# A fused attention and feed-forward kernel: weight rounding, small steps and feed-forward order rearranged

## The chip, the cores and the metric

The kernel runs on one core of one Trainium2 chip. The metric is the device time of one execution in microseconds (us). The core has TensorE (PE, with PEld for its weight loads), VectorE (DVE), ScalarE (ACT), GpSimd (POOL) and SyncE (SP, which issues most DMAs). Every engine works through its own instructions in order; semaphores join them.

## The reference, cut to what matters

`x` and `ctx` are 64 batches of 128 rows by 256 columns. Four residual layers follow each other:

```
x = x + mlstm(layernorm(x), ctx, ctx, gates, out_w)        # 4 heads of 64, log-sigmoid forget gates, head norm
x = x + layernorm(x) @ (ternary(W0) * mean|W0|).T
x = x + softmax((layernorm(x) @ Wq) @ (ctx @ Wk).T / 16) @ (ctx @ Wv)
x = x + bitlinear(silu(bitlinear(h, Wg)) * bitlinear(h, Wu), Wd),  h = layernorm(x)

ternary(w)      = clip(round(w / mean|w|), -1, 1)
bitlinear(x, w) = act_quant(x) @ (ternary(w) * mean|w|).T
act_quant(x)    = round(x * 127 / max|x|) * max|x| / 127   # max over each row
```

Wg and Wu are 1024 x 256, Wd is 256 x 1024. So three large weights are rounded and clipped to -1, 0, 1 once, and in the last layer the rows are rounded twice: before gate and up (256 columns) and after the product (1024 columns).

## The kernel before, in words

The 64 batches are 16 groups of four. `schedule` writes out two opening turns and then 14 turns z = 0 to 13; turn z works on three groups at once: projections and gates of group z+2, decay, scores and heads of group z+1 (m), the two middle layers of group z. It also prepares the quantized rows of group z-1 (y) and stores those of z-2 (w) to a DRAM scratch, `rows_q`. Each engine has the stages of a turn in a fixed written order, and the eight PSUM banks go round in the order of `STAGES`. After turn 13 the last groups are drained, and then 64 feed-forward iterations i run, one per batch.

In a turn VectorE does: statistics of x (L1198), `cut_product`, statistics of group y, `x2_rows`, statistics, `head_sums` (L1321), `row_steps` for y (L1269: maximum, scale, inverse, factors for the way back), one pass of `ternary` (L1233), the gates (L1409 on: sum, negated, absolute value, copy, relu; then, after ScalarE's exp and log, `nlf`, L1421), `row_maxima`, `heads_out`, the running maximum and its splits, `x3_rows`, statistics. ScalarE does the gates' exp and log (L938, L940) behind its copies of stage T2 (L819), and the exponentials of the softmax (L852) behind those.

Weights: `ternary(n, step)` is three VectorE passes over 128 x 2048 floats for each of n = 1 (gate), 2 (up), 3 (down): scale and round, minimum, maximum into a 16-bit tile. Two passes stand in the second opening turn, one in each of turns 0 to 6 (`TERNARY_AT`). TensorE transposes the result in stages WG, WU, WD, at the end of turns 0, 3 and 6 (`WEIGHTS_AT`), and ScalarE copies it out.

Feed-forward iteration i: TensorE does gate and up (`gate_up`, L684 to L690), the transposes of product i-2 (`product_rows`, L699), down of i-3 (`down`, L707). ScalarE: silu (L989), copy of the transposed product i-2 (L993), scaled result of i-3 (L1000). VectorE: product of up and silu (L1513), its row maximum (L1516), step (L1523), its inverse `hscale` (L1526), then `last_rows(i)`, the remaining row work of groups 13 to 15. GpSimd: `hback` (L1145), rounding of the product (L1152), sum with x (L1160). SyncE issues the transposing reads of `rows_q` four iterations ahead and one store of 512 KB for each group, the last one after all four batches are done (L464). The product has two buffers (halves of C), the rounded one too.

## Time and profile before

| | us |
|---|---|
| three timed runs | 701.86, 703.54, 704.52 (median 703.54) |
| the profiled execution's own time | 703.04 |
| its span | 701.3 |
| opening turns, to the first x1 (0 to 47.03) | 47.03 |
| turns 0 to 13 (47.03 to 453.94) | 406.91 |
| draining of the last groups (453.94 to 491.29) | 37.35 |
| feed-forward, first to last product (491.29 to 689.34) | 198.05 |
| after the last product (689.34 to 701.3) | 11.96 |

The boundaries are starts of VectorE's instruction L1359 (x1 of a group; one per turn) and of L1513 (one per feed-forward iteration). 1.7 us of the execution's time lie outside the span.

### The profile page before, as it was taken

The numbers are of one execution on the slowest core, as the hardware profiler recorded it, in microseconds if no ns is written. First come the engines' busy times: TensorE is split into PE (matmuls) and PEld (weight loads), VectorE is DVE, ScalarE is ACT, GpSimd is POOL, SyncE is SP. The second block draws the span as 40 slices with busy tenths as digits, with TensorE's granted clock in tenths as the row PEclk, the third lists the DMA queues.
The fourth block names the chain that finished last, engine by engine and source line by source line (L and its number), as shares of the span: only waits on it lengthen the run. The fifth ranks groups of instructions, "written<-read, shape, count | busy, mean of one in ns | idle before, by whom it ended". The sixth has DMA issues, their size and how long they took to land.

```text
span 701.3 us, 15286 instructions
## 1 busy us (share of the span) xinstructions
PE 655.5 (93%) x4958; PEld 493.9 (70%) x4958; DVE 609.0 (87%) x1661; ACT 518.3 (74%) x1203; POOL 391.8 (56%) x556
## 2 busy tenths in 40 slices
PE   5889999999999999999999999998899999999996
PEld 4668778686867868788787787876465666666664
DVE  4787989888898887989889889897999999999994
ACT  4556677686767668787777787865588889888885
POOL 3366564362735445574574555652366667666665
PEclk9999999999999999999999999999999999999999
DMA  8310202122020312202212121014123424425221
GB/s 290 102 44 18 91 1 92 48 74 90 17 92 16 91 46 76 91 16 91 77 47 91 45 78 61 17 56 155 50 85 94 143 79 122 120 81 158 84 78 61
DMA packets 72659, 55.54 MB, mean 79 GB/s; under 512 B 20093, under 2 KB 72318, under 8 KB 72582
## 3 DMA queue, kind: packets, MB, share of 16 engines
q1 hardware_dynamic: 64134, 50.37, 23.7%
q10 hardware_dynamic: 8448, 4.20, 2.0%
q8 instruction: 42, 0.69, 0.4%
q14 instruction: 35, 0.29, 0.1%
HBM read 29.39 MB, written 20.97 MB: 72 GB/s over the span
## 4 chain that ended last, share of the span: by engine, by line
PE 53%; DVE 30%; ACT 10%; issue 4%; POOL 1%; DMA 1%; DVEq 0%; POOLq 0%; ACTq 0%
PE bank L690 10%; PE bank L637 8%; PE bank L658 8%; PE bank L607 5%; PE bank L707 5%; DVE C L1513 4%; DVE hmax L1516 4%; DVE st L1200 3%; PE bank L679 3%; PE bank L699 3%; PE bank L575 3%; ACT ew L852 2%; PE bank L566 2%; PE bank L512 2%; DVE x L1359 2%
## 5 line engine op out<-in xcount | busy, mean ns | idle before, releaser
L690 PE MATMUL bank<-WGU,fqT 128*128 128x512 bf16 x512 | 125.0, 382 | 4.0 <-DVE C L1513 3.4
L1074 POOL TENSOR_SCALAR_AFFINE_SELECT D<-D 128x512 f32<-128x512 f32 x64 | 38.4, 636 | 124.9 <-ACT D L843 124.9
L1059 POOL TENSOR_TENSOR rs<-ve,minus_half 128x4 f32<-128x4 f32 x64 | 65.3, 1026 | 47.5 <-DVE ve L1206 47.0
L1513 DVE SCALAR_TENSOR_TENSOR C<-bank,fback,D 128x1024 f32<-128x1024 f32 x64 | 81.9, 1280 | 7.4 <-ACT D L989 5.5
L690 PEld LDWEIGHTS bank<-WGU,fqT 128*128 128x128 bf16 x512 | 48.0, 98 | 57.0 <-DVE C L1513 17.3
L989 ACT ACTIVATE D<-bank,fback 128x1024 f32<-128x1024 f32 x64 | 71.1, 1111 | 15.6 <-PE bank L690 15.3
L1516 DVE TENSOR_REDUCE hmax<-C 128x1 f32<-128x1024 f32 x64 | 78.1, 1220 | 2.2
L993 ACT ACTIVATE fhT<-bank 128x1024 f16<-128x1024 f16 x64 | 65.5, 1023 | 19.5 <-PE bank L699 18.2
L1152 POOL TENSOR_SCALAR wtmp<-C,hscale 128x1024 f32<-128x1024 f32 x64 | 71.6, 1119 | 0.4 <-issue 0.4
L707 PE MATMUL bank<-WD,fhT 128*128 128x256 f16 x512 | 66.3, 273 | 0.3 <-ACT fhT L993 0.3
L1200 DVE BATCH_NORM_STATS2 st<-x 128x6 f32<-128x256 f32 x180 | 63.1, 413 | 2.6
L658 PE MATMUL bank<-W0T,x1T 128*128 128x256 f32 x256 | 59.3, 385 | 5.2 <-DVE C L1311 5.2
L637 PEld LDWEIGHTS bank<-vaug,C 128*128 128x128 f32 x512 | 61.6, 194 | 2.3 <-issue 1.6
L637 PE MATMUL bank<-vaug,C 128*128 128x65 f32 x512 | 61.6, 274 | 1.3 <-DVE C L1311 1.3
L607 PE MATMUL bank<-WX,qcT 128*128 128x268 f32 x256 | 62.0, 395 | 0.0
L575 PE MATMUL bank<-qcT,GT 128*128 128x512 f32 x128 | 60.6, 597 | 0.8 <-ACT GT L945 0.8
L1086 POOL TENSOR_TENSOR hr<-hv,minus_half 128x16 f32<-128x16 f32 x16 | 50.5, 3158 | 18.1 <-DVE hv L1340 18.1
L1145 POOL TENSOR_SCALAR hback<-hstep,mean_abs 128x1 f32<-128x1 f32 x64 | 17.2, 268 | 76.1 <-DVE hscale L1526 61.6
L658 PEld LDWEIGHTS bank<-W0T,x1T 128*128 128x128 f32 x256 | 47.3, 190 | 13.9 <-DVE C L1311 7.6
L1080 POOL TENSOR_TENSOR hh<-us,head_scale 128x256 f32<-128x256 f32 x64 | 43.4, 685 | 23.3 <-ACT usq L835 15.3
L1117 POOL TENSOR_TENSOR vaug<-cg,vg 128x256 f32<-128x256 f32 x64 | 50.7, 819 | 8.3 <-ACT vg L888 7.7
L607 PEld LDWEIGHTS bank<-WX,qcT 128*128 128x128 f32 x256 | 47.3, 190 | 11.0 <-issue 3.0
(198 smaller groups left out, 1514.2 us busy)
## 6 DMA issues: line engine op xcount, KB each, us to landing
out_dram<-x SPq DMA_DIRECT2D x31, 512.0 KB, 3.3
xg<-in_x_dram SPq DMA_DIRECT2D x16, 512.0 KB, 3.9
cg<-in_ctx_dram SPq DMA_DIRECT2D x16, 512.0 KB, 4.5
rows_q<-fq ACTq DMA_DIRECT2D x16, 256.0 KB, 2.2
xg<-out_dram SPq DMA_DIRECT2D x8, 512.0 KB, 5.1
cg<-out_dram SPq DMA_DIRECT2D x8, 512.0 KB, 5.0
raw<-in_L_ffn_w_gate_dram SPq DMA_DIRECT2D x1, 1024.0 KB, 7.9
nrm<-in_L_ffn_w_up_dram SPq DMA_DIRECT2D x1, 1024.0 KB, 10.3
```

What stands on the lines that cost most here:

```text
L575: mm = pe.matmul(o[:, :], GT[:, c, rows_at * P:(rows_at + 1) * P], turned[:, EC + c, :, :].rearrange("p b t -> p (b t)"), start=(c == 0), ...
L607: mm = pe.matmul(o[:, 0:VG], qcT[p][:, EC + c, b, :], WX[:, c, :], start=(c == 0), stop=(c == EC - 1))
L637: mm = pe.matmul(o[:, h * AUG:(h + 1) * AUG], C[:, b, h, :], vaug[q][:, b, h, :], start=True, stop=True)
L658: mm = pe.matmul(o[:, 0:E], x1T[:, b, c * P:(c + 1) * P], W0T[:, c, :], start=(c == 0), stop=(c == EC - 1))
L690: mm = pe.matmul(ps[k + half], fqT[:, s, c, :], WGU[:, c, which, half * 512:(half + 1) * 512], start=(c == 0), stop=(c == EC - 1))
L707: mm = pe.matmul(o[:, 0:E], fhT[:, s % 2, c * P:(c + 1) * P], WD[:, c, :], start=(c == 0), stop=(c == IC - 1))
L989: act.activation(fsil[:, s % 2, :], gate, ACT.Silu, scale=fback[:, p, s % FB, 0:1]).then_inc(g_clear, 1)
L993: act.activation(fhT[:, s % 2, :], bank_h[s % 2], ACT.Copy, bias=-OFFSET).then_inc(h_clear, 1)
L1152: pool.tensor_scalar(fhr[:, s % 2, :], fh[:, s % 2, :], hscale[:, s % FB:s % FB + 1], CODE, ALU.mult, ALU.add).then_inc(f_hr, 1)
L1200: dve.bn_stats(st[i][:, b, :], src[:, b, :]).then_inc(stats[i], 1)
L1513: dve.scalar_tensor_tensor(out=fh[:, s % 2, :], in0=up, scalar=fback[:, p, s % FB, 1:2], in1=fsil[:, s % 2, :], op0=ALU.mult, op1=ALU.mult ...
L1516: dve.tensor_reduce(hmax[:, s % FB:s % FB + 1], fh[:, s % 2, :], AX.X, ALU.max, apply_absolute_value=True).then_inc(f_hm, 1)
```

## The change: what it does

- Weights: ScalarE scales and rounds (`weight_rounded`, with the constant CODE so that the low 16 bits hold the value plus 1536); VectorE clips in one pass (`clip`); TensorE transposes the low halves; the copies out subtract 1536. Rounding of 1 and clip 1 stand in the second opening turn, 2 and 3 in turn 0; WG, WU, WD in turns 0, 1, 2.
- Gates: absolute value and relu move to ScalarE, ahead of exp and log.
- Smaller VectorE: one instruction fewer in `head_sums` (the factor 1/64 goes into `head_scale`), two fewer in `row_steps`; the `ve` of statistics 3 moves to GpSimd, ahead of its power.
- Feed-forward: TensorE's order is gate(i), transposes(i-2), up(i), down(i-3). VectorE keeps maximum and reciprocal (a guard column of 1e-5 stands in for the step's maximum); GpSimd multiplies by 127 and by mean/127. The product's buffers are tiles of `vg`.
- Last rows: spread over more iterations, statistics of group 14 before the feed-forward, x3 of group 15 two batches at a time; `rows_q` of groups 13 to 15 stored by SyncE. GpSimd scales two heads before `power(3)` in the draining. The last group is stored batch by batch.

```diff
-WEIGHTS_AT = {0: "WG", 3: "WU", 6: "WD"}
-TERNARY_AT = {0: (1, 2), 1: (2, 0), 2: (2, 1), 3: (2, 2), 4: (3, 0), 5: (3, 1), 6: (3, 2)}
+WEIGHTS_AT = {0: "WG", 1: "WU", 2: "WD"}
...
-        fh = flat(C).rearrange("p (i n) -> p i n", i=2)
+        fh = [flat(vg[k])[:, 0:INNER + 1] for k in (1, 2)]
... sync
+            for s in range(FB):
+                sp.wait_ge(f_done, B - FB + s + 1)
+                sp.dma_start(out[B - FB + s, :, :], fo[(NG - 1) % 2][:, s, :]).then_inc(f_last, 16)
... tensor
+            for i in range(B):
+                if i > 0:
+                    gate_rows_in(i)
+                if i in (2, 3):
+                    last_rows_out(i - 2)
+                if i > 1:
+                    product_rows(i - 2, i % 2)
+                if i > 0:
+                    up_rows_in(i)
+                if i in (3, 4):
+                    last_rows_out(i - 1)
+                if i > 2:
+                    down(i - 3)
... scalar
+                def weight_rounded(n):
+                    if n == 1:
+                        act.wait_ge(means_ready, 1)
+                    act.activation(w_raw[n], w_raw[n], ACT.Identity, scale=mean_inv[:, n:n + 1],
+                                   bias=magic[:, 0:1]).then_inc(w_round, 1)
...
                 if "W0" in bank.stages:
                     weight_copies("W0")
+                    weight_rounded(1)
+                if z == 0:
+                    weight_rounded(2)
                 if y is not None:
                     normalise_rows(y)
...
                 if n is not None:
-                    act.wait_ge(gstep, 4 * n + 3)
+                    act.wait_ge(gstep, n + 1)
+                    act.activation(gabs[:, :, :], gates[:, :, NH:], ACT.Abs).then_inc(g_exp, 1)
+                    act.activation(gneg[:, :, :], gates[:, :, NH:], ACT.Relu, scale=-1.0)
+                    act.wait_ge(g_exp, 2 * n + 1)
                     act.activation(gexp[:, :, :], gabs[:, :, :], ACT.Exp, scale=-1.0).then_inc(g_exp, 1)
...
+                if z == 0:
+                    weight_rounded(3)
                 if y is not None:
                     scale_rows(y, (0, 1))
... gpsimd
+                if i == 3:
+                    pool.wait_ge(aggr[3], GB * group + GB)
+                    pool.tensor_scalar(ve[3][:, :], mv[3][:, :, 1], LN_EPS, 1.0, ALU.add, ALU.mult).then_inc(veps[3], 1)
...
+            def product_scales(i):
+                s = i % FB
+                pool.wait_ge(f_hinv, i + 1)
+                pool.tensor_scalar(hscale[:, s:s + 1], hinv[:, s:s + 1], 127.0, None, ALU.mult).then_inc(f_hs, 1)
+                if i >= FB:
                     pool.wait_ge(o_clear, i - 1)
+                pool.tensor_scalar(hback[:, s:s + 1], hmax[:, s:s + 1], mean_abs[:, 3:4], 1.0 / 127.0,
                                    ALU.mult, ALU.mult).then_inc(f_hback, 1)
... vector
+            def clip(n):
+
+                dve.wait_ge(w_round, n)
+                dve.tensor_scalar(w_raw[n], w_raw[n], CODE + 1.0, CODE - 1.0, ALU.min, ALU.max).then_inc(tern, 1)
...
                 if "WS" in bank.stages:
-                    ternary(1, 0)
-                    ternary(1, 1)
+                    clip(1)
+                if z == 0:
+                    clip(2)
                 if y is not None:
                     row_steps(y)
-                if z in TERNARY_AT:
-                    ternary(*TERNARY_AT[z])
...
+                if z == 0:
+                    clip(3)
                 if z is not None:
                     inverse(bank, z)
                     x3_rows(bank, z, x2, x3)
...
-                for group, src, at in ((NG - 3, None, 1), (NG - 2, x3, 7), (NG - 1, x3_last, 24)):
+                for group, at in ((NG - 3, 2), (NG - 2, 20), (NG - 1, 38)):
+                    if i in range(at, at + 2 * GB, 2):
+                        row_max(group, ((i - at) // 2,))
```

## Rows read from the trace of the kernel before

**Rows 1.** Busy time by turn: stretch, length, then busy us (instructions) per engine, TensorE's granted clock.

```profile
47.03:453.94 406.91, 387.87 (x2958) 313.53 (x2957) 356.40 (x1163) 300.40 (x853) 223.70 (x294) 0.98 0.20 61
...
103.95:133.60 29.65, 27.78 (x210) 22.05 (x210) 26.56 (x85) 21.57 (x63) 15.27 (x21) 1.00 0.19 64
133.60:164.37 30.77, 29.29 (x210) 23.24 (x210) 26.98 (x86) 21.49 (x63) 15.38 (x21) 0.94 0.20 61
...
256.88:286.92 30.04, 29.35 (x221) 23.84 (x222) 24.69 (x84) 23.27 (x65) 15.64 (x21) 0.94 0.20 63
...
426.11:453.94 27.83, 26.97 (x211) 22.00 (x211) 24.61 (x84) 21.72 (x63) 16.14 (x22) 1.00 0.15 49
...
491.29:689.34 198.05, 194.07 (x1484) 122.81 (x1484) 187.46 (x317) 165.05 (x207) 127.71 (x190) 0.99 0.34 97
```

**Rows 2.** The chain of waits through a late turn, 334 to 364: start, us, what.

```profile
339.41 0.22 ACT gexp L938
...
339.65 0.23 ACT glog L940
...
339.97 0.40 DVE nlf L1421
...
340.89 0.28 DVE rawmax L1346
```

**Rows 3.** The chain of waits through turn 1, 74 to 106.

```profile
98.04 1.20 DVE nrm L1236
```

**Rows 4.** TensorE in order of time, end of turn 2.

```profile
133.15 1.62 PE L674 MATMUL bank<-ident,ew 128*128 128x128 f32 x4 [0.67 <-ACT ew L852]
```

**Rows 5.** ScalarE in order of time: the copies of stage WG.

```profile
77.46 1.94 ACT L884 ACTIVATE WGU<-bank 128x1024 bf16<-128x1024 f16 x2 [1.67 <-PE bank L535]
```

**Rows 6.** The draining, in order of time.

```profile
467.80 2.61 POOL L1080 TENSOR_TENSOR hh<-us,head_scale 128x256 f32<-128x256 f32 x4
...
467.93 0.60 DVE L1326 SCALAR_TENSOR_TENSOR hn<-us 128x16 f32<-128x16 f32 x1
```

**Rows 7.** Start of the feed-forward, in order of time.

```profile
491.29 1.28 DVE L1513 SCALAR_TENSOR_TENSOR C<-bank,fback,D 128x1024 f32<-128x1024 f32 x1 [3.56 <-ACT D L989]
...
494.32 1.66 DVE L1371 SCALAR_TENSOR_TENSOR qn<-bank,einv,hh 128x256 f32<-128x256 f32 x4
```

**Rows 8.** Last iterations of the feed-forward, all engines, in order of time.

```profile
686.17 0.26 POOL L1145 TENSOR_SCALAR hback<-hstep,mean_abs 128x1 f32<-128x1 f32 x1 [0.83 <-DVE hscale L1526]
...
686.30 1.28 DVE L1513 SCALAR_TENSOR_TENSOR C<-bank,fback,D 128x1024 f32<-128x1024 f32 x1
...
686.41 1.12 POOL L1152 TENSOR_SCALAR wtmp<-C,hscale 128x1024 f32<-128x1024 f32 x1
...
687.08 1.89 PE L690 MATMUL bank<-WGU,fqT 128*128 128x512 bf16 x8
...
688.14 1.11 ACT L989 ACTIVATE D<-bank,fback 128x1024 f32<-128x1024 f32 x1 [0.34 <-PE bank L690]
...
688.80 0.61 PE L699 MATMUL bank<-ident_h,wtmp 128*128 128x128 f16 x8
688.87 0.15 DVE L1523 TENSOR_SCALAR hstep<-hmax 128x1 f32<-128x1 f32 x1
689.06 0.16 DVE L1526 RECIPROCAL hscale<-hstep 128x1 f32<-128x1 f32 x1
...
689.25 1.04 PE L707 MATMUL bank<-WD,fhT 128*128 128x256 f16 x8
...
690.63 0.62 PE L699 MATMUL bank<-ident_h,wtmp 128*128 128x128 f16 x8 [0.34 <-POOL wtmp L1152]
...
697.92 0.37 SPq L464 DMA_DIRECT2D out_dram<-x  x1
```

**Rows 9.** DMA issues: what, count, KB each, median us to landing.

```profile
out_dram<-x SPq DMA_DIRECT2D x31, 512.0 KB, 3.3
...
rows_q<-fq ACTq DMA_DIRECT2D x16, 256.0 KB, 2.2
```

More of the change, by code:

```diff
@@ L15 @@
 IC = INNER // P
+HEAD_ROOT = 8.0
 AUG = DH + 1
@@ L369, in build @@
         fore, aft = last_places()
-        def feed_forward(eng, turn, behind={}):
-            for g in range(NG):
-                turn(g, g % 4, g == 0, g == NG - 1)
-                if g in behind:
-                    behind[g]()
         @block.sync
@@ L437, in _ @@
             sp.dma_start(grp(out, NG - 1), x3_last[:, :, :]).then_inc(x_out, 16)
-            def rows_written(g):
-                def wait():
-                    sp.wait_ge(q_out, 16 * (g + 1) + 16)
-                return wait
-            def written():
-                sp.wait_ge(x_out, 16 * NG)
-            def turn(g, p, first, last):
-                for s in range(FB):
-                    i = FB * g + s
-                    if not last:
-                        hold("sp", sp, u_full, i + 1)
-                        rows_turned(i + FB, s)
-                    if s == FB - 1 and not first:
-                        sp.wait_ge(f_done, FB * g)
-                        sp.dma_start(grp(out, g - 1), fo[(p + 1) % 2][:, :, :]).then_inc(f_out[(p + 1) % 2], 16)
-                        if g + 3 < NG:
-                            q = (p + 3) % 4
-                            sp.dma_start(fx[q], grp(out, g + 3)).then_inc(f_in[q], 16)
@@ new lines, in ffn_block @@
+            def ffn_block(i):
+                if i + FB < B:
+                    hold("sp", sp, u_full, i + 1)
+                    rows_turned(i + FB, i % FB)
+                if i % FB == FB - 1 and i >= FB:
+                    group_out(i // FB - 1)
+            for i in range(B):
+                for g, at in ((NG - 3, 18), (NG - 2, 36), (NG - 1, 54)):
+                    if i == at:
+                        sp.wait_ge(f_q, g + 1)
+                        sp.dma_start(grp(rows_q, g), fq[:, :, :]).then_inc(q_out, 16)
+                if i == FB * (NG - 6):
+                    sp.wait_ge(x_out, 16 * NG)
+                for g in range(NG - 3, NG):
+                    if i == FB * (g - 1):
+                        sp.wait_ge(q_out, 16 * (g + 1) + 16)
+                ffn_block(i)
@@ L1132, in _ @@
             power(2, NG - 1)
+            power(3, NG - 2)
+            shifts(3, NG - 2)
             def last_rows(i):
-                for group, at in ((NG - 2, 12), (NG - 1, 29)):
-                    if i == at:
-                        power(3, group)
-                        shifts(3, group)
-            def scale_back(i, s):
-                if not isinstance(i, int) or i > 3:
+                if i == 25:
+                    pool.wait_ge(f_n, GB * (NG - 1))
+                    power(3, NG - 1)
+                if i == 27:
+                    shifts(3, NG - 1)
@@ L1162, in ffn_turn @@
-            def ffn_turn(g, p, first, last):
-                for s in range(FB):
-                    i = FB * g + s
-                    scale_back(i, s)
-                    ffn_round(i, s)
-                    if s > 2:
-                        ffn_out(i - 3, s - 3, g, p)
-                    elif not first:
-                        ffn_out(i - 3, s + 1, g - 1, (p - 1) % 4)
-                    last_rows(i)
-            feed_forward(pool, ffn_turn)
-            for s in range(1, FB):
-                ffn_out(B - FB + s, s, NG - 1, 3)
+                pool.tensor_tensor(fo[g % 2][:, s, :], fy[:, i % 2, :], fx[g % 4][:, s, :], ALU.add).then_inc(f_done, 1)
@@ L1178, in _ @@
+            for i in range(B):
+                product_scales(i)
+                ffn_round(i)
+                if i > 2:
+                    ffn_out(i - 3)
+                last_rows(i)
+            for i in range(B - 3, B):
+                ffn_out(i)
         @block.vector
@@ L1390, in turn @@
                     means(bank)
-                    for step in range(3):
-                        ternary(0, step)
+                    ternary_w0()
                 if y is not None:
@@ L1528, in ffn_turn @@
-            def ffn_turn(g, p, first, last):
-                for s in range(FB):
-                    i = FB * g + s
-                    ffn_mul(i, s, g, p % 2)
-                    row_scale(i, s)
-                    if s == 1 and not last:
-                        scales(g + 1, 1 - p % 2)
-                    last_rows(i)
-            feed_forward(dve, ffn_turn)
+                dve.reciprocal(hinv[:, s:s + 1], hmax[:, s:s + 1]).then_inc(f_hinv, 1)
+            for k in range(2):
+                dve.memset(fh[k][:, INNER:INNER + 1], Q_EPS).then_inc(f_guard, 1)
@@ L1541 @@
+            for i in range(B):
+                ffn_mul(i)
+                if i % FB == 1 and i < B - FB:
+                    scales(i // FB + 1, (i // FB + 1) % 2)
+                last_rows(i)
 _INS = ['x', 'ctx_1024', 'L0_xattn_igate_w', 'L0_xattn_igate_b', 'L0_xattn_fgate_w', 'L0_xattn_fgate_b',
```

316 lines of the change are left out of this document (146 added, 170 removed).

## The prediction

> **What bounds the kernel now.** First the busy time by stretch. In the late turns TensorE is busy 26.97 of 27.83 us and VectorE 24.61; in turns with a pass of `ternary` the turn is longer (29.65), and where the clock column says 0.94 longer still (30.77) [rows 1]. So an early turn pays for more than the late one, and the late one is near TensorE's own limit. The feed-forward is 198.05 us for 63 iterations, 3.14 each, with both TensorE (194) and VectorE (187) nearly full [rows 1]. Then the chain of waits, to see which engine's work is really in the path. In a late turn it goes through ScalarE's exp and log to `nlf`, then through VectorE's `rawmax`, with one engine behind the other in every step [rows 2], and stays on VectorE through heads, splits, `x3_rows` and statistics until `cut_product` frees the banks of the next large product. The three or four small VectorE steps ahead of `nlf` are not in it: VectorE waits there for ScalarE. In turn 1 the pass of 1.20 us is in the chain [rows 3]. Last, the order of time in the feed-forward, to see who is late: TensorE starts gate at 687.08, the transposes at 688.80, down at 689.25 and has no gap; its own work takes 1.72 + 0.45 + 0.88 = 3.05 [rows 8]. VectorE's products start at 686.30 and, with the silu of 688.14 ending at 689.25, again near 689.34. VectorE itself could go round faster: the reciprocal starts 2.76 after the product (689.06 - 686.30), and the next product could follow about 0.11 later, 2.87. One row maximum of about 0.3 more makes 3.18, above TensorE's 3.05; that is where 3.14 comes from.
>
> **Opening turns.** `head_sums` loses a step of 0.2 in the chain; two passes become one, but the chain waits there for GpSimd's power. I take -0.4 (bounds -1.5 to +1).
>
> **Turns 0 to 13, weights.** These take 406.91 now [rows 1]. At the late pace of 27.83, thirteen intervals are 361.8, and the first, without a y group, is 26.85: 388.6. So 18.3 us is what weights cost today, for seven passes of about 1.2 (8.4), three transposing stages, and the low clock. After: clip 3 lies in the chain once (+1.2, [rows 3] for the length; it stands between the splits and `x3_rows`, which all lead to `cut_product`). Clip 2 stands where turn 0 waited for the projections: 0, as its cover is TensorE's projection; +1.2 if that cover is gone. WG, WU and WD add some 0.3 each while TensorE waits for VectorE anyway: +0.9 (bounds 0 and 2.2 each, the latter being 30.04 - 27.83 [rows 1], which also holds a low clock). ScalarE's three passes: the nearest row is 1.94 for 2 x 1024 elements [rows 5], so 1.94 each. Two stand in the slot that `normalise_rows` fills in later turns, and empty here, or beside queued copies; the third pushes the exponentials of turn 0 by 0.5, under VectorE's splits. I take +0.2 for all; bounds 0 and 5.8. The low clock: 30.77 - 29.65 = 1.1 a turn in four turns [rows 1], all with the wait of 0.67 ahead of the transposes of `ew` [rows 4]; I expect it gone. Sum of weights after: 1.2 + 0.9 + 0.2 = 2.3, so -16.0.
>
> A rule of the Trainium skill speaks against this part: "ScalarE: Activation LUTs", "Rules for kernel authors", puts relu, max, min, add and mul on VectorE rather than ScalarE. The rows agree on the length of one pass (1.94 against 1.20 [rows 3, 5]). They differ on what counts: ScalarE is busy 21.6 of 29.65, VectorE 26.6. By the rule the three passes would cost +5.8 and the time would be near 690; it is weighed as a rival below.
>
> **Gates.** Abs and relu on ScalarE stand behind the same copies and ahead of exp. Relu is pipelined; exp has to wait for abs, and one such dependent step is 339.65 - 339.41 = 0.24 [rows 2]. VectorE gives up three steps of 0.2, but it waited for the log anyway, so nothing comes back. `nlf` starts 0.25 late; of that the last `rawmax` had 0.07 of slack: it starts 0.18 late and everything behind it too. 13 turns x 0.18 = +2.3 (bounds -0.2 a turn, if the copies come earlier, and +0.3). The lighter `head_sums`, `row_steps` and `ve` save VectorE about 0.5 a turn, but lie ahead of the wait for the log: 0. The trace has no abs and no relu on ScalarE; the table sets are a risk (below). Turns together: -16.0 + 2.3 = -13.7.
>
> **Draining.** VectorE's four small steps of `head_sums` take 0.60 each beside GpSimd's 2.61 us of head scaling [rows 6], and 0.2 elsewhere. With two of the four scalings moved ahead of the power, about two of these steps fall back to 0.2, and one step goes: -1.0 (bounds -1.8 and 0). The statistics of group 14 (1.9 us) come in where VectorE waits 3.56 us for the first silu [rows 7]: 0, and +1.9 if that wait is gone.
>
> **Feed-forward.** Start: between product 0 and product 1 stand the four x3 rows, 494.32 to 495.98, so that the second comes 4.8 after the first (491.29) [rows 7]; two at a time makes 3.76 (2.68, 0.25 for the inverse, 0.83) and then 3.5. VectorE after: reciprocal at 2.57, next product at 2.68, with one row step 2.99, under 3.05. So its extras are free, and TensorE's 3.05 remains. But the new order makes a loop that had slack before: the transposes of product i now stand ahead of up(i+2). Its parts: up to product 1.06, as gate to silu (688.14 - 687.08); product to transposes 690.63 - 686.30 = 4.33 as a chain today; from this one VectorE step of 0.19 goes (689.06 - 688.87), and GpSimd's multiplication by 127 comes in with 0.24 (686.41 - 686.17, hback to rounding) plus the handoff, so +0.2, 4.53; transposes 0.45 (689.25 - 688.80). All [rows 8]. 1.06 + 4.53 + 0.45 = 6.04 in two iterations against TensorE's 6.10. It just fits, with nothing to spare. Before, the same transposes stood one up later and had 1.3 us. So now whatever delays one product or rounding is paid in full: three times ScalarE's conversion of a group's rows (1.05 us; silu 0.4 late), once GpSimd's power (1.0 us): I take 3 x 0.36 + 0.6 + 0.7 for small ones = 2.4. Product 0 to 63: 3.76 + 3.5 + 3.0 + 3.1 + 59 x 3.05 + 2.4 = 195.7, against 198.05: -2.4. Bounds: -5 (no delay paid) and, if the loop takes 6.3 rather than 6.04, +3.5.
>
> **End.** From the last product to its transposes +0.2. The last store starts at 697.92 and carries 512 KB; such stores land in 3.3 us, 256 KB of `rows_q` in 2.2 [rows 8, 9]. 1.1 less for half the size puts 128 KB near 1.7; the three before it are still on the queue, so I take -1.2 (bounds 0 and -1.7).
>
> **Sum.** -0.4 - 13.7 - 1.0 - 2.4 + 0.2 - 1.2 = -18.5 on the profiled execution's 703.04: 684.5. The median of the runs is 0.5 above that execution, so 685.0.
>
> **Rivals.** (a) The feed-forward loop is too long: the handoffs between three engines are worth 0.1 to 0.2 more per iteration than the rows of a relaxed loop say, and VectorE's row steps are then paid again. For it: 6.04 against 6.10. Against: every part is a row. 63 x 0.12 = +7.5, 692.5. (b) ScalarE's passes, clip 2 and the three transposing stages are in the path, as they are put close together: 5.8 + 1.2 + about 1 = +8, 693. For it: ScalarE's order is fixed and vg copies and exponentials stand behind each pass; against: its slots in turn 0 were partly empty. (c) The other side: a clock drop in every turn. Place: the transposes of `ew`. The longer gate chain delays the exponentials in all turns; TensorE waits, and a part of the turn then goes at the lower of its two levels, 1.2 instead of 2.4 GHz, as the clock column's 0.94 says of turns today [rows 1]. Price: 1.1 for the drop and about 0.6 for the wait in each of 14 turns, 23.8, 708.5. It decides when the wait reaches the 0.67 us of [rows 4]; the late turns, with 0.18 more, should stay under it. (d) The change does not do what it says: abs or relu needs another activation table: two loads a turn at 1.28 us, the length of the profile's two table loads, 14 x 2.56 = +36, 721. The same page of the Trainium skill ("Table sets: the hidden batching unit") says that cheap functions such as relu and abs are in every set, and prices a switch at about 2.7 us; no run here shows it. (e) Everything fits: extras in the feed-forward hidden, the gate chain's 0.18 absorbed, -5 more: 680.
>
> **How the numbers follow.** Forecast 0.58, (a) 0.14, (b) 0.12, (c) 0.05, (d) 0.02, (e) 0.09. The forecast's own range is 681 to 690. From 679 to 696, (e), (a) and (b) are in and about 0.15 is left out. A measurement of this kernel tells 0.5% (3.5 us) from no change: faster needs under 700.0. All but (c), (d) and mixtures of (a) and (b) with a partial (c) are faster: 0.92, same 0.03, slower 0.05.
>
> **What would show it.** Turns 3 to 13 at 28.0, clock 1.00; turn 1 near 29.4; `nlf` still waiting for the log, its wait longer; no table load in the turns; the feed-forward at 3.05 with jumps only at the three conversions and one power, GpSimd's rounding the last releaser of the transposes; the last store landing in about 2 us. Wrong if late turns fall below 27.8 (then VectorE's small steps were in the path), if turns stay at 29 or more, or if products stand 3.15 apart.

## The result

The changed kernel takes 684.0 us (median of 4 runs, 682.09 to 684.74) against 702.9 for the kernel before on the same chip: ratio 0.9725, 95% interval 0.9695 to 0.9755. Forecast were 685.0, range 679 to 696, faster. The profiled execution took 683.39, with a span of 681.4 (before 703.04 and 701.3).

| stretch | before | after | difference | forecast |
|---|---|---|---|---|
| opening, to the first x1 | 47.03 | 45.08 | -1.95 | -0.4 |
| turns 0 to 13 | 406.91 | 390.07 | -16.84 | -13.7 |
| draining, to the last x1 | 21.83 | 20.74 | -1.09 | -1.0 |
| last x1 to the first product | 15.52 | 17.06 | +1.54 | 0 |
| first to last product | 198.05 | 197.49 | -0.56 | -2.4 |
| after the last product | 11.96 | 10.96 | -1.0 | -1.0 |

(x1 and the product are the two instructions of VectorE whose starts mark the stretches; the last x1, that of group 15, begins at 475.77 in before: 453.94 to 475.77 and 475.77 to 491.29.)

Busy time by stretch in the kernel after, the same columns as [rows 1]: length, then busy us (instructions) of PE, PEld, DVE, ACT, POOL, granted clock, DMA share, GB/s. The rows are all turns, turn 1, turn 2, a late turn, and the feed-forward.

```profile
45.08:435.15 390.07, 379.83 (x2961) 309.03 (x2960) 330.49 (x1064) 304.85 (x883) 212.52 (x305) 1.00 0.20 63
71.39:100.59 29.20, 28.10 (x227) 22.88 (x226) 24.84 (x78) 22.04 (x64) 15.27 (x22) 1.00 0.17 56
100.59:129.45 28.86, 28.23 (x227) 23.04 (x226) 24.22 (x78) 23.46 (x67) 15.25 (x22) 1.00 0.20 65
213.54:241.17 27.63, 27.17 (x212) 22.04 (x211) 23.66 (x77) 21.64 (x65) 15.26 (x22) 1.00 0.23 67
472.95:670.44 197.49, 191.83 (x1485) 121.12 (x1484) 176.15 (x238) 164.76 (x208) 140.40 (x253) 1.00 0.34 97
```

Four readings. The clock is 1.00 in every turn, where four turns of before had 0.94 or 0.95. The turns reach the late pace (that of the turns in which no weight work is left) from turn 4 on, but for turn 8 with 28.21. That pace is 27.63, below the 27.84 of before, where the forecast had 28.0. In the feed-forward VectorE lost 11 us of work, TensorE 2, and the time barely moved.

### The profile page after: what moved, and what is told of

Read it like the earlier page. It is cut to its first block, busy times and chain, and to the rows that moved or that the text cites. A ratio compares the mean times of both kernels' runs of the same rounds, so it can differ in the third digit from the quotient of the medians.

```text
span 681.4 us, 15144 instructions
## 1 busy us (share of the span) xinstructions
PE 645.2 (95%) x4958; PEld 487.7 (72%) x4958; DVE 570.5 (84%) x1481; ACT 524.6 (77%) x1238; POOL 395.2 (58%) x636
## 4 chain that ended last, share of the span: by engine, by line
PE 68%; DVE 15%; ACT 10%; issue 3%; POOL 2%; DMA 1%; POOLq 0%; DVEq 0%; SPq 0%; ACTq 0%
PE bank L603 9%; PE bank L654 8%; PE bank L633 8%; PE bank L693 7%; PE bank L685 6%; PE bank L709 6%; PE bank L701 4%; PE bank L675 4%; ACT ew L853 4%; PE bank L508 3%; PE bank L571 3%; ACT x2T L820 2%; PE bank L562 2%; DVE st L1215 2%; PE bank L647 2%
## 5 line engine op out<-in xcount | busy, mean ns | idle before, releaser
L1520 DVE SCALAR_TENSOR_TENSOR vg<-bank,fback,D 128x1024 f32<-128x1024 f32 x64 | 82.1, 1283 | 18.2 <-PE bank L693 15.4
L1527 DVE TENSOR_REDUCE hmax<-vg 128x1 f32<-128x1025 f32 x64 | 78.1, 1221 | 2.2
L1172 POOL TENSOR_SCALAR wtmp<-vg,hscale 128x1024 f32<-128x1024 f32 x64 | 71.9, 1123 | 5.8
L685 PE MATMUL bank<-WGU,fqT 128*128 128x512 bf16 x256 | 65.7, 379 | 2.0 <-DMA fqT<-rows_q 1.6
L693 PE MATMUL bank<-WGU,fqT 128*128 128x512 bf16 x256 | 65.7, 379 | 0.0
L709 PEld LDWEIGHTS bank<-WD,fhT 128*128 128x128 f16 x512 | 49.9, 98 | 19.3 <-issue 0.6
L1099 POOL TENSOR_TENSOR hr<-hv,minus_half 128x16 f32<-128x16 f32 x16 | 46.5, 2905 | 14.8 <-DVE hv L1349 14.7
L867 ACT ACTIVATE qn<-xg,shift,rs 128x256 f32<-128x256 f32 x64 | 33.2, 593 | 26.9 <-POOL shift L1079 26.9
```

Of the source, the lines that this page charges most:

```text
L685: mm = pe.matmul(ps[bG + half], fqT[:, i % FB, c, :], WGU[:, c, 0, half * 512:(half + 1) * 512], start=(c == 0), stop=(c == EC - 1))
L693: mm = pe.matmul(ps[bU + half], fqT[:, i % FB, c, :], WGU[:, c, 1, half * 512:(half + 1) * 512], start=(c == 0), stop=(c == EC - 1))
L709: mm = pe.matmul(o[:, 0:E], fhT[:, i % 2, c * P:(c + 1) * P], WD[:, c, :], start=(c == 0), stop=(c == IC - 1))
L1172: pool.tensor_scalar(fhr[:, i % 2, :], fh[i % 2][:, 0:INNER], hscale[:, i % FB:i % FB + 1], CODE, ALU.mult, ALU.add).then_inc(f_hr, 1)
L1520: dve.scalar_tensor_tensor(out=fh[i % 2][:, 0:INNER], in0=up, scalar=fback[:, g % 2, s, 1:2], in1=fsil[:, i % 2, :], op0=ALU.mult, op1=ALU ...
L1527: dve.tensor_reduce(hmax[:, s:s + 1], fh[i % 2], AX.X, ALU.max, apply_absolute_value=True).then_inc(f_hm, 1)
```

## The experiments

Each was run four times, e1 to e4 on one chip and e5 to e12 on another, always beside the kernel before, whose median was 702.05, 702.22 and 702.80 in the three rounds. Kernels of different rounds are best compared by the ratio. The times of e2, e5, e6, e7 and e8 overlap the range of the kernel after; what these five show is read from the stretches of their profiled executions, one for each kernel. Boundaries are starts of the same instructions as above.

| kernel | us (range of 4) | ratio to before | opening | turns | to last x1 | to product 0 | products |
|---|---|---|---|---|---|---|---|
| before | | | 47.03 | 406.91 | 21.83 | 15.52 | 198.05 |
| after | 684.0 (682.1 to 684.7) | 0.9725 | 45.08 | 390.07 | 20.74 | 17.06 | 197.49 |
| e1 gates on ScalarE | 693.32 (692.5 to 694.0) | 0.9868 | 45.56 | 395.90 | 22.17 | 17.05 | 199.45 |
| e2 gates back on VectorE | 683.96 (683.7 to 685.1) | 0.9742 | 47.20 | 389.50 | 20.42 | 17.04 | 197.17 |
| e3 weights alone | 688.10 (687.6 to 688.7) | 0.9795 | 46.53 | 391.11 | 21.82 | 15.52 | 199.88 |
| e4 old order of TensorE | 680.84 (680.1 to 681.6) | 0.9697 | 45.34 | 389.96 | 20.74 | 17.05 | 194.24 |
| e5 early reads | 682.36 (681.8 to 684.5) | 0.9711 | 48.41 | 389.43 | 20.74 | 16.91 | 196.16 |
| e6 last group whole | 684.25 (683.9 to 685.3) | 0.9746 | 45.90 | 390.14 | 20.73 | 15.52 | 197.55 |
| e7 draining order back | 684.56 (682.9 to 685.1) | 0.9740 | 45.59 | 389.75 | 21.70 | 16.96 | 197.55 |
| e8 hback after rounding | 682.09 (681.6 to 682.9) | 0.9713 | 45.01 | 389.73 | 20.74 | 17.05 | 196.58 |
| e9 weights and gates | 684.98 (684.9 to 687.4) | 0.9754 | 44.83 | 391.08 | 21.82 | 15.68 | 197.90 |
| e10 old order, early reads | 680.47 (679.9 to 681.1) | 0.9677 | 46.04 | 389.94 | 20.74 | 17.21 | 194.24 |
| e11 and hback late | 680.36 (679.8 to 680.9) | 0.9679 | 45.40 | 389.93 | 20.74 | 17.05 | 194.25 |
| e12 and gates by turn | 677.11 (676.7 to 677.8) | 0.9633 | 45.70 | 388.86 | 20.73 | 15.52 | 193.74 |

### The turns: weights, gates, small steps (e1, e2, e3, e9)

e1 is the kernel before with the gates' part alone:

```diff
-                    act.wait_ge(gstep, 4 * n + 3)
+                    act.wait_ge(gstep, n + 1)
+                    act.activation(gabs[:, :, :], gates[:, :, NH:], ACT.Abs).then_inc(g_exp, 1)
+                    act.activation(gneg[:, :, :], gates[:, :, NH:], ACT.Relu, scale=-1.0)
```

> The kernel before with only the gates' absolute value and relu moved to ScalarE. Theory A (contention): VectorE idles while GpSimd centres vaug, so vaug takes near 2.3 us instead of 3.4 and x1 1.23 instead of 1.52; late turns 27.6 us instead of 27.83, some 1.5 to 3 us off the kernel's time. Rival B (what the prediction said): nlf starts 0.25 later and the turn gets 0.18 longer, late turns 28.0, the kernel 2 us slower. Rival C: the shorter late turn comes from the lighter head_sums and row_steps, not from the gates; then late turns are 27.8 to 28.0 here.

e2 is the kernel after with the same lines turned back (VectorE has its three steps again).

> The changed kernel with the gates' absolute value and relu back on VectorE. Theory A: vaug near 3.4 us again, x1 1.5, late turns 27.7 to 27.9 although nlf starts 0.2 earlier; the kernel 1 to 3 us slower than the changed one. Rival B: late turns 27.4, 2.5 us faster than the changed one. Rival C (lighter VectorE steps alone do it): late turns stay at 27.6.

e3 is the kernel before with the weights' part alone:

```diff
-TERNARY_AT = {0: (1, 2), 1: (2, 0), 2: (2, 1), 3: (2, 2), 4: (3, 0), 5: (3, 1), 6: (3, 2)}
+                def weight_rounded(n):
+                    act.activation(w_raw[n], w_raw[n], ACT.Identity, scale=mean_inv[:, n:n + 1],
```

> The kernel before with only the weight part: rounding on ScalarE, one clip each on VectorE, transposing stages in turns 0, 1 and 2. Theory: the weights are the bulk of the gain. Turns 0 to 13 take 406.9 - 16 = about 391, turns 4 to 13 are 27.83 each, granted clock 1.00 in all of them, the opening turns lose 1 to 1.5 us (GpSimd's power of the heads 2.9 us instead of 3.9 next to fewer VectorE passes); the kernel near 686. Rival: the low clock in four turns is not due to the weight passes and stays; then 391 + 4 x 1.1 = 395 and near 690.

e9 is e1 and e3 in one kernel.

> The kernel before, with two parts of the change alone: the weights (rounded on ScalarE, one clip, WG, WU, WD in turns 0 to 2) and the gates' absolute value and relu on ScalarE. The lighter head_sums and row_steps, ve on GpSimd, the feed-forward, the draining and the end are those of before. Question: why is a late turn 27.63 in the kernel after, when gates on ScalarE alone gave 27.83 and the kernel after without that edit gave 27.80. Theory: it needs both the shorter VectorE steps (GpSimd's vaug then runs alone, 2.34 instead of 3.40 us) and the gates on ScalarE; with the gates alone a late turn stays at 27.8, the turns (first to last x1) near 391.5 and the time at 688. Rival: weights and gates are enough, the smaller edits are worth nothing: 27.63, turns 390, time 686.8. In both cases the two edits do not add up: weights alone gave -15.8 us in the turns, gates alone -11.0.

Measured in the turns: weights alone -15.80, where -16.0 was forecast; gates alone -11.01, where a small loss was forecast; both together -15.83. So the gates are worth 11 us beside `ternary` and nothing without it (391.08 against 391.11). The four kernels without `ternary` in the turns separate the two other parts:

| turns, us | gates on VectorE | gates on ScalarE |
|---|---|---|
| weights alone | 391.11 (e3) | 391.08 (e9) |
| and all smaller edits | 389.50 (e2) | 390.07 (after) |

The smaller edits (lighter `head_sums` and `row_steps`, `ve` of statistics 3 on GpSimd) are worth 1.6 and 1.0, the gates 0.0 and +0.6. No run has one of the smaller edits by itself.

Against the expectations: none for e1 had the 11 us (theory A had at most 3); its late turns are 27.83, as in its rival C, and `vaug` still takes 3.4. In e2 `vaug` takes 2.34, where its theory A had 3.4; its late turns are 27.80 as in A, but its time is that of the kernel after and not longer, as its first four turns are shorter. e3 has the turns as expected and the clock 1.00 in them, but its opening lost only 0.5 and its time is 2 above the 686 expected. e9 has late turns and turns as in its theory, at a time 3 below the expected 688.

Why the gates are worth 11 us beside `ternary`: in turn 4 of the kernel before, VectorE in order of time (start, us, engine line, operation):

```profile
190.60 1.28 DVE L1236 TENSOR_SCALAR wtmp<-wtmp,mean_inv 128x2048 f32<-128x2048 f32 x1
191.91 0.48 DVE L1410 TENSOR_TENSOR gates<-vg,gate_q 128x32 f32<-128x32 f32 x1
192.43 0.52 DVE L1412 TENSOR_SCALAR gneg<-gates 128x16 f32<-128x16 f32 x1
192.99 0.53 DVE L1414 TENSOR_TENSOR gabs<-gates,gneg 128x16 f32<-128x16 f32 x1
193.44 0.20 DVE L1415 COPY igr<-gates 128x96 f32<-128x96 f32 x1
193.56 0.58 DVE L1417 TENSOR_SCALAR gneg<-gneg 128x16 f32<-128x16 f32 x1
194.18 0.26 DVE L1421 TENSOR_TENSOR nlf<-gneg,glog 128x96 f32<-128x96 f32 x1
```

and in e1 the same place:

```profile
183.33 1.28 DVE L1239 TENSOR_SCALAR wtmp<-wtmp,mean_inv 128x2048 f32<-128x2048 f32 x1
184.65 0.48 DVE L1413 TENSOR_TENSOR gates<-vg,gate_q 128x32 f32<-128x32 f32 x1
185.16 0.56 DVE L1415 COPY igr<-gates 128x96 f32<-128x96 f32 x1
185.91 0.43 DVE L1419 TENSOR_TENSOR nlf<-gneg,glog 128x96 f32<-128x96 f32 x1 [0.19 <-ACT glog L943]
```

The pass pushes the gates to where GpSimd's `vaug` runs. There the 16-column steps take 0.5 to 0.6 and end 0.03 behind a piece of it; in turns without a pass they stand beside `hr` and take 0.17. From the pass's start to the end of `nlf` it is 3.84 before and 3.01 in e1, and `nlf` waits for nothing before: the steps were in the path. The wait of TensorE ahead of the transposes of `ew` falls too:

```profile
163.92 1.62 PE L674 MATMUL bank<-ident,ew 128*128 128x128 f32 x4 [0.67 <-ACT ew L852]
...
196.32 1.62 PE L674 MATMUL bank<-ident,ew 128*128 128x128 f32 x4 [0.83 <-ACT ew L852]
```

are rows of before (ends of turns 3 and 4). e1 has, at the end of turn 4,

```profile
188.06 1.62 PE L674 MATMUL bank<-ident,ew 128*128 128x128 f32 x4 [0.35 <-ACT ew L852]
```

and the clock is 1.00 in every turn of it. The wait alone doesn't decide on the clock, though: in before the waits of 0.67 at the ends of turns 2, 3, 5 and 6 are followed by the low clock, that of 0.67 at the end of turn 1 and that of 0.83 above are not. At the forecast's 1.1 a turn the four drops make 4.4 of the 11 us, an estimate; how the rest divides between the steps and the wait no run shows.

### The late turn

A late turn takes 27.84 in before and e3, 27.83 in e1 and e9, 27.80 in e2, and 27.63 turn after turn only where the smaller VectorE steps and the gates on ScalarE are together. (Single turns of e1, e2 and e3 leave this pace, as 28.41 and 27.24 one behind the other in e3; what one turn of such a pair gains the other mostly loses.) TensorE's own rows show where: the first line is e9, where each late turn has this wait, the second is turn 8 of the kernel after, the only late turn of it that takes 28.21.

```profile
335.04 3.72 PE L659 MATMUL bank<-W0T,x1T 128*128 128x256 f32 x16 [0.58 <-DVE C L1332]
```

```profile
279.27 3.72 PE L654 MATMUL bank<-W0T,x1T 128*128 128x256 f32 x16 [0.58 <-DVE C L1322]
```

In the other late turns of the kernel after, this wait for `cut_product` is not there. What stands ahead of that product on VectorE, and what GpSimd does then, in turn 8:

```profile
278.06 0.56 DVE L1221 TENSOR_SCALAR ve<-mv 128x4 f32<-128x4 f32 x1
278.54 2.47 DVE L1322 TENSOR_TENSOR C<-bank,D 128x512 f32<-128x512 f32 x4
```

```profile
277.96 0.64 POOL L1087 TENSOR_SCALAR_AFFINE_SELECT D<-D 128x512 f32<-128x512 f32 x1
```

and in turn 9:

```profile
306.00 0.25 DVE L1221 TENSOR_SCALAR ve<-mv 128x4 f32<-128x4 f32 x1
306.17 2.47 DVE L1322 TENSOR_TENSOR C<-bank,D 128x512 f32<-128x512 f32 x4
```

```profile
305.60 0.64 POOL L1087 TENSOR_SCALAR_AFFINE_SELECT D<-D 128x512 f32<-128x512 f32 x1
```

The mask instruction ends at 278.60 and 306.24; `ve`, of 4 columns, ends at 278.62 and 306.25. The small step is held until the mask instruction that was running is over: begun 0.1 after its start it takes 0.56, begun 0.4 after it 0.25. The fourteen traces have 326 such steps begun inside a mask instruction or a piece of GpSimd's head scaling, more than 0.1 before its end; 325 end 0.02 to 0.04 behind it. Beside GpSimd's `rs`, its power, it isn't so: at 395.42 in e1, begun 0.16 into an `rs` of 1.01, `ve` takes 0.17. The Trainium skill, "SBUF — State Buffer", "Who interferes with whom", says that the two engines share a port pair under an exclusive lock, and that a VectorE instruction in a mode with two ports and GpSimd's block each other for the whole instruction, whichever came second; the rows beside the mask and the scaling agree.

So 0.3 us more or less in VectorE's order ahead of the product decides on TensorE's 0.58, and turn 8 is longer than its neighbours by just that. This is read from the rows; no run isolates it. With the gates alone (e9) `ve` begins 0.12 into the mask, with the smaller edits alone (e2) 0.15, with both 0.41. How a wait of 0.58 less makes a steady turn shorter by only 0.21 isn't shown, nor what sets off turn 8.

### The feed-forward (e4, e5, e8, e10, e11)

The distance to product n is the time from the start of product n-1 to that of n. e4 is the kernel after with TensorE's order of before, gate, up, transposes, down:

```diff
+                if i > 0:
+                    up_rows_in(i)
                 if i in (2, 3):
                     last_rows_out(i - 2)
                 if i > 1:
                     product_rows(i - 2, i % 2)
-                if i > 0:
-                    up_rows_in(i)
```

> The changed kernel with TensorE's order gate, up, transposes, down as before; all else as changed. Theory (a loop without slack): the loop over product, maximum, inverse, two GpSimd steps, rounding and transposes gets about 1.3 us of slack, so GpSimd's power (3.9 instead of 3.05 between two products) is hidden; conversions still cost 0.4 each; steady spacing 3.05; product 0 to 63 takes 1 to 2 us less, and the end after the last product 0.9 to 1.1 less of its own by the later up. Rival: the old order makes VectorE's products wait for up behind a late u_clear, spacing 3.1 or more, 2 us or more slower.

Measured: first to last product 194.24 instead of 197.49, and 680.84. The new order costs 3.2 us, more than the 1 to 2 expected, and everything else in the feed-forward brings 3.8 over before. Of the 3.2, 1.34 is one distance, that to product 4 (3.00 instead of 4.34), and 1.91 lies behind it (180.65 instead of 182.56). The conversions cost about as much in e4 (3.51, 2.68, 3.29 at the first), the power 0.66 less (3.22 for 3.88). The end after the last product stays at 10.95; the 0.9 to 1.1 expected there didn't come. e5 keeps the new order and moves two reads:

```diff
             store(NG - 2)
+            for i in range(2):
+                hold("sp", sp, u_full, i + 1)
+                rows_turned(i + FB, i)
             sp.wait_ge(x3_ready, GB * NG)
...
-                if i + FB < B:
+                if 2 <= i and i + FB < B:
```

> The kernel after, but SyncE issues the transposing reads of rows 4 and 5 of the feed-forward ahead of the last store of x3 (group 15), so that they no longer stand behind its wait for VectorE. Theory: gate(4) of the kernel after waits 1.61 us for the read that SyncE issues only at 480.92, right behind that store; product 4 follows product 3 after 4.34 instead of 3.0 to 3.1, and in the relaxed loop nothing makes this good. Then here the wait is gone, that distance is near 3.0, first to last product 196.2 instead of 197.5, and the time 682.7. Rival: the row itself is late in landing because of other traffic on the queues (the store of 512 KB, the loads of x), or TensorE's new order makes the jump (transposes of product 2 wait for the rounding): then the distance stays at 4.2 to 4.4, and the time at 684.0.

Measured: the distance to product 4 is 3.14 instead of 4.34, and first to last product 196.16 instead of 197.49, as its theory had it. The kernel after, SyncE's and TensorE's rows (SPq: issue of a DMA):

```profile
480.41 0.38 SPq L431 DMA_DIRECT2D out_dram<-qn  x1
480.92 17.32 SPq L420 DMA_TRANSPOSE fqT<-rows_q  x8
```

```profile
485.43 1.04 PE L685 MATMUL bank<-WGU,fqT 128*128 128x512 bf16 x4 [1.61 <-DMA fqT<-rows_q]
```

and e5:

```profile
474.44 4.69 SPq L420 DMA_TRANSPOSE fqT<-rows_q  x2
482.94 0.38 SPq L434 DMA_DIRECT2D out_dram<-qn  x1
```

The read needs nothing but free rows in `fqT`, which it had at 474.4 in e5. In program order it stood behind a store that waits for VectorE's last x3; TensorE went on 4.5 us after its issue.

e8 keeps the new order and shortens GpSimd's way to the rounding:

```diff
                 ffn_round(i)
+                product_back(i)
```

> The kernel after (TensorE's order gate, transposes, up, down), but GpSimd computes hback, the factor for the way back, behind the rounding of the product instead of ahead of it. Theory: the loop product, maximum, inverse, GpSimd's two small steps (0.21 and 0.27 us), rounding, transposes, up is as long as two iterations of TensorE, so that what it is shortened by returns where something delays it: every conversion and the power of GpSimd cost 0.2 less, the iterations between stay near 3.06 instead of 3.08; first to last product 196.5 instead of 197.5 (bounds 195.5 and 197.2), the time 683.0. Rival: the loop has slack in the plain iterations and the jumps come from ScalarE's conversions alone, whatever GpSimd does: then 197.4 and 684.0. A second one: hback is now late for ScalarE's scaled result of the same product, or GpSimd's sum with x is pushed back: above 197.7.

Measured: 196.58 and 682.09, as its theory had it; behind product 4 it is 1.04 less (181.52). The long distance that ends each conversion goes from 3.42, 3.39 and 3.45 to 3.28, 3.22 and 3.27, one iteration in four from 3.08 to 3.05; the power still costs (3.80 for 3.88). The loop through GpSimd is the limit in the new order. e10 is e4 with the early reads, e11 that with the late `hback`.

> The kernel after with TensorE's order of before in the feed-forward (gate, up, transposes, down) and the reads of rows 4 and 5 ahead of the last store of x3. Theory: in the old order gate(4) stands 0.6 us later and its read had landed just in time (product 4 came 3.00 after product 3), so the earlier read adds nothing: first to last product 194.2, the time 680.8. Rival: the start still pays something for the read; then up to 0.3 us less, 193.9 and 680.5. If the gain of 1.3 us of the new order came on top, 192.9 and 679.5, the reason given for gate(4)'s wait is wrong.

> As the previous one (old order of TensorE, early reads), and GpSimd's hback behind the rounding. Theory: in the old order the loop through GpSimd has slack of one up (0.87 us), so that shortening it by 0.27 us gives nothing in plain iterations (3.06 with hback ahead) and little at the conversions: first to last product 193.8 to 194.3, the time 680.7. Rival: GpSimd's way is in the path here as well, and the full 0.9 us of the same edit in the new order comes back: 193.3, the time 679.9.

Measured: 194.24 and 194.25, as e4, and 680.47 and 680.36: the theories. Against e5 the new order by itself costs 1.92 (196.16 and 194.24, both with early reads). Both edits, worth 1.33 and 0.91 us in the new order, are worth nothing in the old one, where the transposes stand one up (0.87 us) later and gate(4) finds its row. What the new order asks for is seen in the waits of the kernel after, 500 to 680 (total us, times, longest):

```profile
PEld bank L701 <- POOL wtmp L1172: 20.3, 53, 1.8
DVE vg L1520 <- PE bank L693: 14.1, 37, 1.1
```

53 times in some 56 iterations the weight load of the transposes is held up by GpSimd's rounding. In before the first place in that view was GpSimd waiting for VectorE:

```profile
POOL hback L1145 <- DVE hscale L1526: 56.5, 53, 2.1
```

### End and draining (e6, e7)

```diff
-            for s in range(FB):
-                sp.wait_ge(f_done, B - FB + s + 1)
-                sp.dma_start(out[B - FB + s, :, :], fo[(NG - 1) % 2][:, s, :]).then_inc(f_last, 16)
+            sp.wait_ge(f_done, B)
+            sp.dma_start(grp(out, NG - 1), fo[(NG - 1) % 2][:, :, :]).then_inc(f_out[(NG - 1) % 2], 16)
```

> The kernel after, but the last group of four batches is stored whole after its last batch (512 KB), as before, not batch by batch (128 KB each). Theory: the 1.0 us between the last product and the end (10.96 after, 11.96 before) is the difference in landing of a store of 512 and one of 128 KB: the end goes back to 11.9 to 12.0 and the time to 685.0. Rival: the microsecond comes from the order at the end (down and transposes of the last iterations) or from GpSimd's shorter work there: then the end stays near 11.0 and the time at 684.0.

Measured: the end takes 12.06 (681.9 - 669.84) instead of 10.96, as its theory had it. The time, 684.25, is not the 685.0 expected; the profiled execution has no drop in clock at the last x1 (15.52 instead of 17.06). In the kernel after the four stores of 128 KB land in 2.1 us each, those of 512 KB in 3.1 (the lines answer to [rows 9]):

```profile
out_dram<-x SPq DMA_DIRECT2D x6, 512.0 KB, 3.1
...
out_dram<-x SPq DMA_DIRECT2D x4, 128.0 KB, 2.1
```

e7 puts all four head scalings behind the power again:

```diff
             power(1, NG - 2)
-            scale_heads(fore, 0)
-            scale_heads(fore, 1)
             power(3, NG - 3)
```

> The kernel after, but in the draining GpSimd does its power and shifts for statistics 3 first and then all four head scalings, as before. Theory: the two scalings moved ahead of the power took VectorE's small steps of head_sums out of the shared stretch; undone, the way from the end of turn 13 to the last x1 grows by 0.6 to 1.1 us (20.74 to about 21.6), and the time to about 684.9. The drop of TensorE's clock near 458 us stays, since it comes after a wait of 2.4 us for x1 which this edit does not touch: from the last x1 to product 0 it stays at 17.0. Rival: the order of GpSimd's work in the draining is what brought the drop in clock (the kernel before had none there, 15.5 us from the last x1 to product 0): then that stretch goes back to 15.5 and the time falls to about 683.4.

Measured: 21.70 instead of 20.74 to the last x1, as forecast, and the stretch behind it stays at 16.96: GpSimd's order isn't what brings the low clock there.

### The clock

Windows of 2 us behind the last x1, same columns as above, first the kernel after, then e12:

```profile
456.00:458.00 2.00, 0.73 (x4) 0.76 (x5) 1.97 (x4) 0.09 (x1) 0.72 (x1) 0.84 0.03 6
458.00:460.00 2.00, 2.00 (x9) 1.82 (x8) 1.82 (x11) 1.45 (x4) 0.63 (x1) 0.50 0.62 151
460.00:462.00 2.00, 2.00 (x9) 1.67 (x8) 1.03 (x5) 1.70 (x8) 0.39 (x1) 0.81 1.09 375
```

```profile
458.00:460.00 2.00, 2.00 (x11) 1.77 (x10) 1.76 (x12) 0.62 (x3) 1.02 (x1) 1.00 0.82 264
460.00:462.00 2.00, 1.94 (x13) 1.53 (x12) 1.69 (x5) 2.00 (x11) 0.00 (x0) 1.00 1.09 363
```

Both follow the same wait of TensorE for x1:

```profile
457.27 1.89 PE L647 MATMUL bank<-ident,x 128*128 128x128 f32 x8 [2.36 <-DVE x L1368]
```

```profile
456.66 1.06 PE L651 MATMUL bank<-ident,x 128*128 128x128 f32 x8 [2.37 <-DVE x L1382]
```

In the first the eight transposes run at the lower of the two levels, 1.2 GHz, and take 1.89 instead of 1.06. The stretch to product 0 is 16.9 to 17.2 in nine profiled kernels and 15.5 to 15.7 in five (before, e3, e6, e9, e12), among them kernels with either draining; e6 differs from the kernel after in nothing that comes before it. So the drop belongs to no edit tried here; what decides on it no run isolates. The Trainium skill, "TensorE: Matmul & The Clock Gate", "What's actually happening", has the gate watch a window that runs freely, not from the kernel's start; that the same code comes with the drop and without it agrees with this. The opening is alike: at 32 to 36 us the clock is 0.62 to 0.64 in before, e3, e5 and e6 and 1.00 in the others. e1 and e3 have another drop at the start of the feed-forward, of 7 us (0.50 in e3 from 482 to 486), which makes their third and fourth distances 4.2 and 3.6 instead of the 3.14 and 3.15 of e9; that is 1.5 of the 1.6 and 2.0 us by which their products take longer. Before has a shorter one there (0.50 from 497.5 to 500.5), and its first four distances are only 0.1 longer than those of e9.

### Gates on VectorE in four turns (e12)

e12 is e11 with one edit more:

```diff
+GATES_DVE = (2, 3, 4, 5)
...
+                    if n in GATES_DVE:
+                        dve.tensor_scalar(gneg[:, :, :], gates[:, :, NH:], -1.0, None, ALU.mult).then_inc(gstep, 1)
+                        dve.wait_ge(gstep, before_n + 2)
+                        dve.tensor_tensor(gabs[:, :, :], gates[:, :, NH:], gneg[:, :, :], ALU.max).then_inc(gstep, 1)
```

> As the previous one, and the gates' absolute value and relu on VectorE in turns 0 to 3 alone (groups 2 to 5), on ScalarE in the opening and in the later turns. Theory: the kernel after with all gates on VectorE had the first four intervals shorter by 0.38, 0.26, 0.45, 0.42 (1.5 in all) and the late ones longer by 0.17 each; taking the better of both by turn gives turns of 388.6 instead of 390.1, and 1.5 us less than the previous kernel: 679.2. Rival: those 1.5 us belonged to the longer opening of that kernel (47.20 instead of 45.08 to the first x1), work that only shifted: then turns of 390.1 and no difference to the previous kernel.

Measured: 677.11, ratio to before 0.9633 (0.9616 to 0.965), 3.2 less than e11. The first four intervals are 26.23, 28.93, 28.43, 28.50 against 26.31, 29.20, 28.84, 28.84, and the turns take 388.86, 1.07 less (1.5 expected). Another 1.53 comes from the way to product 0 without a drop in clock, and 0.5 in the feed-forward, most of it in one conversion (3.50 for 3.78) and in the first distance (3.64 for 3.81). Only the 1.07 is what the edit was made for. Three of e12's four executions have the mean clock of the profiled one, 0.999, and all four (676.7 to 677.8) are below e11's (679.8 to 680.9, clock 0.996 or 0.997), so the missing drop isn't the luck of one execution. Whether it would stay away in another kernel isn't known.

## Why the prediction was right, point by point

**Turns, weights: right in size.** -15.80 in e3 against -16.0. The low clock went, the `ternary` passes went, and the turns of e3 are 2.5 over the 388.6 of the late pace, where 2.3 was forecast: rival (b) fell, and with it the +5.8 that the forecast had drawn from the rule of the Trainium skill ("ScalarE: Activation LUTs", "Rules for kernel authors"). The kernel after has the same two table loads of 1.28 us as before, none in the turns, so rival (d) fell too.

**Turns, gates and smaller edits: both terms missed, by 3.3 together.** The steps that failed are "+2.3" for the gates, which cost 0.0 (e3 to e9) or 0.6 (e2 to after), and "0" for the lighter `head_sums`, `row_steps` and `ve`, which gave 1.6 (e3 to e2) or 1.0 (e9 to after). The forecast had named the sign of this itself: late turns below 27.8 would mean that VectorE's small steps were in the path. They came at 27.63.

In the late turn VectorE waits longer for the log, as forecast (1.09 instead of 0.40 ahead of `nlf`), but the rest differs. With the gates alone (e9 against e3) the log starts 0.14 later, not 0.25, `nlf` 0.07 later, and it ends as before, so that `negmax` and x1 start at the same time: there was no delay to pass on. With the smaller edits the gates do cost something on the way: from e2 to the kernel after `negmax` starts 0.45 later, but x1 ends only 0.08 later, as the `hh` between them takes 1.21 in after and 1.66 in e2, where it begins beside `vaug`. That `vaug` takes 2.34 where it took 3.40, and VectorE's x1 1.23 where it took 1.52, comes with the smaller edits and not with the gates: it is 3.39 in e9 and 2.34 in e2. From e2 to after the gates cost 0.3 to 0.5 in each of the first four turns and give 0.17 in most of the late ones. The forecast had priced a chain of fixed durations; what the rows show is a balance of which small step meets which GpSimd instruction.

```profile
321.71 0.70 DVE L1424 TENSOR_TENSOR nlf<-gneg,glog 128x96 f32<-128x96 f32 x1 [1.09 <-ACT glog L953]
```

```profile
321.11 2.34 POOL L1130 TENSOR_TENSOR vaug<-cg,vg 128x256 f32<-128x256 f32 x4
```

```profile
339.64 3.40 POOL L1117 TENSOR_TENSOR vaug<-cg,vg 128x256 f32<-128x256 f32 x4
```

```profile
321.62 3.39 POOL L1132 TENSOR_TENSOR vaug<-cg,vg 128x256 f32<-128x256 f32 x4
```

```profile
322.04 2.34 POOL L1127 TENSOR_TENSOR vaug<-cg,vg 128x256 f32<-128x256 f32 x4
```

(the first two are a late turn of the kernel after, the others those of before [rows 2], of e9 and of e2).

**Opening: -1.95 for -0.4.** The forecast had no term for two parts of it. The gates are one: from the first gate sum to the first `cut_product` it is 11.11 in before, 11.10 to 11.11 in e2 and e3, and 10.39 to 10.41 in the eleven kernels with the gates on ScalarE, so 0.7 is a gain of the change. The other is before's drop in clock at 32 us: from that `cut_product` to the second gate sum it is 13.03 in e6, with the drop, and 12.05 in the kernel after, with the same code there, so about 1.0 is no gain. Another 0.5 is the weights (13.55 in before, 13.03 in e3, both with the drop). The first gate sum itself starts anywhere from 19.1 to 20.3, and in e5, whose low clock lasts 10 us, the opening takes 48.41.

**Draining: right** (-1.09, and e7 gives back 0.96), **but +1.54 behind it was not in the sum**: the drop in clock after the wait of 2.36. The forecast had weighed a drop at the transposes of `ew` in every turn (rival (c)), and not one at a longer wait. Its sign for that drop, a wait that reaches 0.67, isn't borne out either: two such waits of before are followed by none.

**Feed-forward: mechanism right, start missed.** The loop without slack is there: with the old order the products behind product 4 take 1.9 less (e4; 1.8 in e10 against e5), with `hback` out of the way 1.0 less (e8). Products 4 to 63 took 182.56, forecast 59 x 3.05 + 2.4 = 182.35. That these agree so well is in part luck: the three conversions cost about 1.6, not 1.1, the power 0.8, not 0.6, and the small delays 0.2, not 0.7. The failed term is the start: 3.80 + 3.82 + 2.97 + 4.34 = 14.93 instead of 13.36. 1.2 to 1.3 of it is the read behind SyncE's wait (e5), a queue that the forecast did not follow; the rest is the third x3 pair (3.82 for 3.5). The second product of before comes 4.90 after the first, where the forecast read 4.8.

**End: right**, -1.0 for -1.0. The stores of 128 KB landed in 2.1, near the sign of 2, and e6 gives the 1.1 back.

The terms missed by +1.5 and +1.8 on one side and -1.6 and -3.1 on the other. That the total came within 1 us of the forecast is luck: it was better than its terms.

## What to carry to other kernels

When small VectorE steps take 0.5 where their kind takes 0.17, look at what GpSimd runs beside them: here they ended with its mask, scaling or `vaug` instruction. Moving them to a third engine pays in full if they are in the path, and nothing once something else has taken them out of it; so price two such edits together, not one by one. Before putting a stage earlier in TensorE's order, add up the loop that closes through the other engines; and before believing a forecast at a seam, read the DMA queue's order for an independent transfer behind an issue that waits.

## What the runs showed of the hardware

- A 4-column VectorE step ends within 0.04 us of the GpSimd mask or scaling instruction during which it began, in 325 of 326 cases (0.56 and 0.25 long in the rows above; 0.17 alone, and 0.17 beside `rs`).
- The same wait of TensorE (2.36 and 2.37) was followed by the lower clock in one kernel and not in another. Such a drop costs 1.5 us there and 1.0 in the opening (4.1 where it lasts 10 us, in e5); at the start of the feed-forward one of 7 us costs 1.45 (4.18 + 3.56 in e3, 3.14 + 3.15 in e9) and a shorter one 0.1 (before). The profiled executions have between none (e9, clock 0.999, and e12) and six (before, 0.983) of them.
- ScalarE's pass over 2048 columns takes 2.08, little more than the 1.94 of 2 x 1024 in [rows 5]:

```profile
38.09 2.08 ACT L890 ACTIVATE raw<-raw,magic,mean_inv 128x2048 f32<-128x2048 f32 x1
...
68.33 2.08 ACT L890 ACTIVATE wtmp<-wtmp,magic,mean_inv 128x2048 f32<-128x2048 f32 x1
```
